# Decoder layer on one core: softmax inverses spread over rows by DMA through DRAM instead of by matmul

## The reference, cut to what matters

```python
qh, kh, vh = (_split_heads(q), _split_heads(k), _split_heads(v))   # 16 heads of 16
scores = jnp.einsum('bhqd,bhkd->bhqk', qh, kh) * scale
attn = jax.nn.softmax(scores, axis=-1)
ctx = jnp.einsum('bhqk,bhkd->bhqd', attn, vh)
ctx = ctx.transpose(0, 2, 1, 3).reshape(x_q.shape[0], x_q.shape[1], D)
return ctx @ W_out.T + b_out
```

## Time and profile before

| | us |
|---|---|
| median of three runs | 714.04 |
| span of the profiled execution, first to last instruction | 712.5 |
| what lies around the span, by that median | 1.5 |
| attention loop, from the first pair's projection to the last scores | 479 to 583 |
| feed-forward, from the first `hidden` to the end | 594 to 712 |

### The profile page before, as it was taken

How to read it: one execution, slowest core, us unless ns; L and a number is a source line. 1 busy time by engine, 2 the same in 40 slices (tenths; PEclk the granted TensorE clock), 3 DMA queues, 4 the chain that set the end, 5 groups by cost and what they waited for, 6 DMA issues and landing times. The chain is left out here.

```text
span 712.5 us, 12566 instructions
## 1 busy us (share of the span) xinstructions
PE 672.1 (94%) x4412; PEld 491.7 (69%) x4412; DVE 633.6 (89%) x1259; ACT 374.0 (52%) x722; POOL 353.7 (50%) x491
## 2 busy tenths in 40 slices
PE   9889999999989998899999799799999999999995
PEld 3478765887747886468886586567877776666664
DVE  4998787999989999989999979748999996999997
ACT  4732157031255503463232633669777776888885
POOL 0633424646135762158451571391692224788785
PEclk9999999999999999999999999999999999999998
DMA  8630045232522436143663065730000000000012
GB/s 311 180 61 1 0 119 104 74 60 25 64 51 38 104 133 60 29 89 60 192 104 74 0 197 88 256 100 2 2 3 2 2 2 1 1 31 31 32 60 90
DMA packets 35353, 50.51 MB, mean 71 GB/s; under 512 B 4857, under 2 KB 29433, under 8 KB 35035
## 3 DMA queue, kind: packets, MB, share of 16 engines
q0 software_dynamic: 7680, 16.77, 15.1%
q1 hardware_dynamic: 26746, 32.15, 13.9%
q10 hardware_dynamic: 864, 0.79, 0.4%
HBM read 29.79 MB, written 7.34 MB: 52 GB/s over the span
## 5 line engine op out<-in xcount | busy, mean ns | idle before, releaser
L744 ACT ACTIVATE yb<-banks 128x256 f32<-128x256 f32 x64 | 24.2, 386 | 149.2 <-PE banks L445 104.1
L470 PE MATMUL banks<-xt_in,w_in 128*128 128x512 f32 x192 | 87.9, 611 | 0.2
L436 PE MATMUL banks<-inv_m,spec_y 128*128 128x256 f32 x384 | 85.5, 379 | 0.0
L390 PE MATMUL banks<-z_cplx,fwd_m 128*128 128x256 f32 x240 | 72.2, 382 | 9.7 <-DVE prod L1130 5.4
L436 PEld LDWEIGHTS banks<-inv_m,spec_y 128*128 128x128 f32 x384 | 73.0, 190 | 9.9
L391 PE MATMUL banks<-z_cplx,fwd_m 128*128 128x256 f32 x240 | 71.4, 379 | 0.0
L470 PEld LDWEIGHTS banks<-xt_in,w_in 128*128 128x128 f32 x192 | 36.7, 194 | 43.3 <-issue 39.8
L390 PEld LDWEIGHTS banks<-z_cplx,fwd_m 128*128 128x128 f32 x240 | 44.8, 190 | 19.0 <-issue 8.4
L391 PEld LDWEIGHTS banks<-z_cplx,fwd_m 128*128 128x128 f32 x240 | 45.6, 190 | 6.2
L1816 ACT ACTIVATE silu<-ps_score,gate_back 128x1024 f32<-128x1024 f32 x32 | 35.6, 1114 | 19.0 <-issue 17.5
L1786 ACT ACTIVATE prob_t<-ps_pt 128x1024 f32<-128x1024 f32 x32 | 32.7, 1022 | 24.1 <-PE ps_pt L1591 24.1
(11 more groups left out here) (299 smaller groups left out, 1726.7 us busy)
## 6 DMA issues: line engine op xcount, KB each, us to landing
x_tok<-in_x SPq DMA_DIRECT2D x8, 512.0 KB, 4.2
x_tok<-in_b_out POOLq DMA_DIRECT2D x8, 512.0 KB, 13.7
v_t<-left POOLq DMA_DIRECT2D x8, 511.5 KB, 4.5
x_t<-left POOLq DMA_DIRECT2D x8, 511.5 KB, 5.3
xt_in<-in_x_t SPq DMA_DIRECT2D x3, 1024.0 KB, 5.9
x_scratch<-x_tok SPq DMA_DIRECT2D x6, 512.0 KB, 4.0
x<-x_scratch SPq DMA_DIRECT2D x6, 512.0 KB, 9.3
out<-x SPq DMA_DIRECT2D x6, 512.0 KB, 2.9
```

The lines of the kernel that those rows point to most:

```text
L390: mm(o, fwd_m[:, at + 2 * half + odd, :], zz[:, 0, :], start=True, stop=False)
L436: last = mm(bank[:, odd * 2 * P:(odd + 1) * 2 * P], spec_y[:, j + odd, part * D + h * P:part * D + (h + 1) * P], inv_m[:, o:o + 2 * P], st ...
L470: last = mm(proj_pair(b, t)[:, c * 512:(c + 1) * 512], w_in[:, k, TILES[t] * P:(TILES[t] + 1) * P], xt_in[:, k, c * 512:(c + 1) * 512], st ...
```

## The change

The inverses no longer go through TensorE. SyncE writes `inv_sum` to a scratch tensor in DRAM (each row four times) and reads it back with each row on 16 partitions, into `inv_all`. ScalarE copies the contexts (`evac_context`) out of PSUM where it copied the spread inverses. The multiplication moves from VectorE to GpSimd (`multiply(i)`). `project(i)` comes a pair later, so residuals and squares do too. GpSimd's order is written anew: bias, multiplications, quantizing and norms take turns. `quantize` is cut into single passes (not shown), two `x_peak` move from the attention loop to steps 0 and 1 of the feed-forward, and the `spread` constant goes (its load not shown).

```diff
@@ -113,14 +113,10 @@
     for r in range(STRIPS):
-        key_head[:, r] = np.arange(STRIP) % HEADS_T == (2 * r + row // NCTX)[:, None]
-    spread = np.zeros((P, STRIPS, P), f)
-    for g in range(STRIPS):
-        spread[g * STRIP:g * STRIP + HEADS_T, g] = row // DH == np.arange(HEADS_T)[:, None]
+        key_head[:, r] = np.arange(STRIP) // REPS == (2 * r + row // NCTX)[:, None]
     out = {
...
         "c_ident": np.eye(P), "c_pairmask": pair_mask, "c_keyhead": key_head.reshape(P, -1),
-        "c_spread": spread.reshape(P, -1),
     }
@@ -1311,14 +1307,18 @@
 X_ROWS = CHUNKS - CHUNKS_B
-X_LATE, X_EARLY = 12, 5
+CHUNKS_EARLY = 4
+X_LATE, X_EARLY = 14, 5
 W_TILE = 11
-X_SLOTS = {3 + n * 5 // 3: n + X_EARLY * CH for n in range(TILES_ALL - X_EARLY * CH)}
+X_LOOP = TILES_ALL - X_LATE
+X_SLOTS = {n: n + X_LOOP for n in range(X_EARLY * CH - X_LOOP)}
+X_SLOTS.update({3 + n * 5 // 3: n + X_EARLY * CH for n in range(TILES_ALL - X_EARLY * CH)})
 HALF = INNER // 2
...
 STRIPS = P // STRIP
+REPS = STRIP // HEADS_T
 FT = INNER // P
@@ -1438,8 +1435,10 @@
         inv_sum = sb("inv_sum", [P, P])
-        inv_all = sb("inv_all", [P, DT * 2 * P])
-        c_t = sb("c_t", [P, DT, 2 * P])
+        late_rows = x_t[:].rearrange("p c t n -> p (c t) n")
+        inv_all, c_raw = late_rows[:, 0:2], late_rows[:, 2:4]
+        c_t = sb("c_t", [P, 2, DT, 2 * P])
+        inv_dram = [nc.dram_tensor(f"inv_scratch_{n}", [P, REPS, P], F32).ap() for n in range(2)]
         row_sum = sb("a_row_sum", [P, 2, CH]); row_var = sb("a_row_var", [P, 2, CH]); spread_sq = sb("a_spread_sq", [P, D])
@@ -1493,7 +1492,7 @@
                 return ps_score[:, INNER + (i - LAST + 1) * 512:INNER + (i - LAST + 1) * 512 + D]
-            return (ps_ctx, ps_inv)[i % 2][:, 0:D]
+            return (ps_inv, ps_ctx)[i % 2][:, 0:D]
@@ -1501,6 +1500,9 @@
+        def ps_project(i):
+            return ps_inv if i == HALVES - 2 else ps_ctx
         def late_order(c):
@@ -1524,6 +1526,21 @@
+            def spread_inverses(i):
+                sp.wait_ge(inverted, i + 1)
+                if i >= 2:
+                    sp.wait_ge(inv_spread, 16 * (i - 1))
+                rows = inv_dram[i % 2]
+                sp.dma_start(rows, inv_sum[:].unsqueeze(1).broadcast_to([P, REPS, P])).then_inc(inv_written, 16)
+                sp.wait_ge(inv_written, 16 * (i + 1))
+                if i >= 2:
+                    sp.wait_ge(ct_ready, i - 1)
+                sp.dma_start(inv_all[:, i % 2].rearrange("p (g n) -> p g n", n=P),
+                             rows.rearrange("(g m) c n -> (m c) g n", g=STRIPS)).then_inc(inv_spread, 16)
...
+            for i in range(HALVES):
+                spread_inverses(i)
             def store(i0, i1):
@@ -1593,26 +1610,20 @@
             def sums(i):
                 pe.wait_ge(pt_evac, 2 * i + 2)
-                pe.wait_ge(inv_evac, i) if i else pe.wait_ge(q_evac, DT * (CHUNKS - Q_EARLY) - 1)
+                pe.wait_ge(inverted, i) if i else pe.wait_ge(q_evac, DT * (CHUNKS - Q_EARLY) - 1)
                 for r in range(STRIPS):
                     for g in range(STRIPS):
-                        k, t = g // DT, g % DT
+                        t, k = g // 2, g % 2
                         last = mm(ps_inv[g * STRIP:(g + 1) * STRIP, 0:P], key_head[:, r, :],
...
-            def spread_inverses(i):
-                pe.wait_ge(inverted, i + 1)
-                for t in range(DT):
-                    for k in range(2):
-                        o = t * 2 * P + k * P
-                        last = mm(ps_inv[:, o:o + P], spread[:, k * DT + t, :], inv_sum[:], start=True, stop=True)
-                last.then_inc(spread_mm, 1)
...
             def values(i):
+                if i >= 2:
+                    pe.wait_ge(added, i - 1)
                 if i:
-                    pe.wait_ge(added, i)
+                    pe.wait_ge(ctx_evac, i)
                 else:
@@ -1625,9 +1636,12 @@
             def project(i):
                 pe.wait_ge(ct_ready, i + 1)
+                pe.wait_ge(inverted, HALVES) if i == HALVES - 2 else pe.wait_ge(ctx_evac, min(i + 2, HALVES))
+                if i == HALVES - 1:
+                    pe.wait_ge(added, HALVES - 2)
                 for k in range(2):
                     for t in range(DT):
-                        last = mm(ps_ctx[:, k * D:(k + 1) * D], c_t[:, t, k * P:(k + 1) * P], wo[:, t, :],
+                        last = mm(ps_project(i)[:, k * D:(k + 1) * D], c_t[:, i % 2, t, k * P:(k + 1) * P], wo[:, t, :],
                                   start=(t == 0), stop=(t == DT - 1))
@@ -1699,12 +1713,11 @@
                 if j % 2 == 0:
-                    if j >= 4:
-                        project(j // 2 - 2)
+                    if j >= 6:
+                        project(j // 2 - 3)
                     if j >= 2:
...
                 elif j >= 3:
-                    spread_inverses(j // 2 - 1)
                     if j == TILES_ALL - 1:
@@ -1716,8 +1729,7 @@
             turn_input(1)
-            project(HALVES - 2)
-            spread_inverses(HALVES - 1)
+            project(HALVES - 3)
             for s in range(TILES_ALL + 3):
@@ -1732,11 +1744,12 @@
                     values(HALVES - 1)
-                if s == 1:
+                    project(HALVES - 2)
+                if s == 2:
                     project(HALVES - 1)
                 if s - 3 in tiles:
-                    if s == 3:
-                        pe.wait_ge(added, HALVES)
+                    if s in (3, 4):
+                        pe.wait_ge(added, HALVES - 4 + s)
                     down(s - 3, FT // 2 if s - 3 == LAST - 1 else 0)
@@ -1786,11 +1799,11 @@
-            def evac_inverses(i):
-                act.wait_ge(spread_mm, i + 1)
-                if i:
-                    act.wait_ge(ct_ready, i)
-                fn(inv_all[:], ps_inv[:], ACT.Copy).then_inc(inv_evac, 1)
+            def evac_context(i):
+                act.wait_ge(pv_mm, i + 1)
+                if i >= 2:
+                    act.wait_ge(ct_ready, i - 1)
+                fn(c_raw[:, i % 2], ps_ctx[:], ACT.Copy).then_inc(ctx_evac, 1)
             def squares(i):
@@ -1857,27 +1870,27 @@
                 if j % 2 and j >= 3:
-                    evac_inverses(j // 2 - 1)
-                if j % 2 == 0 and j >= 6:
-                    squares(j // 2 - 3)
+                    evac_context(j // 2 - 1)
+                if j % 2 == 0 and j >= 8:
+                    squares(j // 2 - 4)
             evac_input(0)
...
             evac_input(1)
-            squares(HALVES - 3)
-            evac_inverses(HALVES - 1)
+            squares(HALVES - 4)
             for s in range(TILES_ALL):
...
                 if s == 0:
-                    squares(HALVES - 2)
+                    evac_context(HALVES - 1)
+                    squares(HALVES - 3)
                 if s - 2 in tiles:
                     evac_hidden(s - 2)
-                if s == 2:
-                    squares(HALVES - 1)
+                if s in (2, 3):
+                    squares(HALVES - 4 + s)
                 if s - 4 in range(LAST - 4):
@@ -1935,8 +1948,12 @@
             pool.wait_ge(ld_kv, 16 * KV_LOADS)
-            for c in range(CHUNKS):
-                add_bias(c)
+            def multiply(i):
+                pool.wait_ge(inv_spread, 16 * (i + 1))
+                pool.wait_ge(ctx_evac, i + 1)
+                if i >= 2:
+                    pool.wait_ge(wo_mm, i - 1)
+                tt(c_t[:, i % 2].rearrange("p t n -> p (t n)"), c_raw[:, i % 2], inv_all[:, i % 2], ALU.mult).then_inc(ct_ready, 1)
             def norm_tile(c, k):
@@ -2020,17 +2041,21 @@
-            norm_chunk(0)
-            pool.wait_ge(w_scaled, 1)
-            quantize(0, w_gate)
-            norm_chunk(1)
-            quantize(1, w_up)
-            quantize(2, w_down)
-            for c in range(2, CHUNKS - 2):
-                norm_chunk(c)
+            for c in range(CHUNKS_EARLY):
+                add_bias(c)
+            for j in range(4, TILES_ALL):
+                if j % 2 == 0:
+                    multiply(j // 2 - 2)
+                    if j < 4 + 2 * (CHUNKS - CHUNKS_EARLY):
+                        add_bias(CHUNKS_EARLY + j // 2 - 2)
+                elif j - W_TILE - 2 in range(18):
+                    quantize((j - W_TILE - 2) // 6, (j - W_TILE - 2) // 2 % 3)
+                if j % CH == 2 and j >= 10:
+                    norm_chunk((j - 10) // CH)
             round_x(0)
...
             back_scales(0)
+            multiply(HALVES - 2)
             round_x(2)
@@ -2041,6 +2066,8 @@
+                if s == 0:
+                    multiply(HALVES - 1)
                 if s in (0, CH):
@@ -2097,15 +2124,8 @@
             def invert(i):
...
                 if i:
-                    dve.wait_ge(spread_mm, i)
+                    dve.wait_ge(inv_written, 16 * i)
                 nc.vector.reciprocal(inv_sum[:], ps_inv[:, 0:P]).then_inc(inverted, 1)
...
-            def normalize(i):
```

(61 more changed lines are left out.)

4 lines of the change are left out of this document (2 added, 2 removed).

## The result

The changed kernel takes 716.53 us (median of seven runs, 715.87 to 719.55) against 714.04 for the one before: ratio 1.0041, 95% interval 1.0026 to 1.0057. It is slower by 2.5 us; the forecast was 2.3. The profiled execution took 718.67 (span 716.9), 2.1 above the median.

A forecast was written before the change was run, and what follows sets the result against it. It took a 7.99 us cycle through TensorE and VectorE to bound the attention loop. With the start's 1.1 gain already counted, 1.6 + 0.5 + 0.2 = +2.3 us on 714.04 gave 716.3 us, range 710.5 to 720.

The forecast's parts named there:

- The ring bounds the loop; spreads and `c_t` are worth nothing: Attention loop: 7.99 us cycle of odd scores, sums, `invert`, even shift sets the pair; removing both pieces gains under 0.1.
- The start, 1.1: First pair, its projection issued a pair later: 6.6 to 6.7 us against 8.0, ScalarE taking 0.2 back; gain 1.1 us.
- 0 for the rest of the loop, 1.2 either way: Twelve attention-loop pairs: removed spreads and `c_t` together change nothing, with 0.1 us a pair, 1.2 us, either way.
- T: Start of the attention loop's last scores: 582.53 before the change, forecast at about 581.4.
- DMA 6.2: Write and read of the inverses through DRAM: 2.6 and 3.4 plus 0.2 for signals, 6.2 us (4.6 to 9.0).
- The hand-over, +1.6: Attention loop to feed-forward: first input tile waits for GpSimd, turned at 590.9 to 591.0 instead of 589.37, +1.6 us.
- Turned input to `hidden(0)`, +0.5: Feed-forward's beginning: 5.0 us instead of 4.47, because the context copy stands ahead of the input copy; +0.5 us.
- `hidden(0)` to `hidden(4)`, 15.7: Feed-forward's first steps: last spread goes, a third projection, residual and two `x_peak` come; 15.7 us against 15.5, +0.2.
- it needs `values` instead of the spread: ScalarE in the loop: swaps one 128x512 copy for another, whose input ends at about the same time; costs nothing.
- the shortening loop (706.7): Rival: VectorE's own sum limits the attention loop, 0.8 us saved a pair, 9.6 in all, total 706.7; chance 0.20.
- The round trip beyond its cover: Rival: inverses' DMAs outlast the loop time hiding them, from 10.8 us; at 13, total about 735; chance 0.08.
- The clock: Rival: TensorE, idling 0.9 in 8 us, drops to 1.2 GHz in the loop; total about 773; chance 0.02.

The follow-up runs named there:

- the first experiment: Changed kernel with round_x(0), round_x(1) and back_scales(0) moved on GpSimd ahead of pair 13's multiplication and the loop's last norm: 713.71 us, ratio 0.9995.

## Why the prediction was right, and where its steps were not

- *The ring bounds the loop; spreads and `c_t` are worth nothing.* Right, shown three ways: ordinary pairs of 8.0 with TensorE idle 0.7 to 0.8 (forecast 0.9) and `prob` as releaser; three quarters of the spreads gone for nothing; VectorE's slot filled for nothing.
- *The start, 1.1.* 1.33 (8.00 to 6.67).
- *0 for the rest of the loop, 1.2 either way.* From 484.45 to T it is 97.63 against 97.11: +0.5. Inside are two pairs longer by 0.68 and 0.49, through `x_unit` beside the multiplication, and ten of 8.05 in the mean, against 8.09 before. The size fell inside my bound; the cause was not in the text. I had costed GpSimd's new work by its room ("per pair 1.2, ... of 8") and never asked beside which VectorE instruction it falls.
- *DMA 6.2.* 2.6 and 2.8; 5.5 us from the write's issue to the multiplication, inside 4.6 to 9.0. The read was over-sized (3.4), because I leaned on the 512 KB loads for its many pieces. The Trainium skill, "DMA: Bandwidth & Descriptors", Anatomy of one DMA — SWDGE (gpsimd) path, gives a fixed 2.0 us plus the bytes at 436 GB/s. An estimate from it is 2.6 for each, and the traces come within 0.2. But that section is on DMAs that GpSimd issues, and these are SyncE's, which the prediction did not say; the nearness is no proof that the formula holds for them.
- *The hand-over, +1.6.* +1.9 (591.29 against 589.37), with every link of the chain as named. T was 0.7 later than I had it, and the multiplication started 0.1 later (585.24 against 585.1) in spite of the quicker DMAs. The squares, priced as the other bound, were only 0.4 behind. The second write's one for one, and the early rounding's full return, show that it is this chain and no other.
- *Turned input to `hidden(0)`, +0.5.* This step failed in the profiled execution: 7.04 instead of 5.0. The 5.0 was laid out at full clock, and there it is right: 4.87 in the first experiment. In the profiled run `values` and `sums` took 0.87 and 0.85 more, and the first `inner` ran slow in part. I had set the fall of the clock beside a stretch busy 18.38 of 22 us and asked it only of the loop, not of the one idle stretch of over 3 us that my own steps contain. The profiled run is 2.1 over the median of its kernel, of the same size. Its mean clock over the run was 0.988 and that of the other long run (719.55) 0.990, against 0.992 to 0.994 in the five from 715.87 to 717.30, so most runs probably keep the clock; their traces were not taken, and this stays an inference. Why some fall and others do not is open.
- *`hidden(0)` to `hidden(4)`, 15.7.* 15.91.
- *ScalarE: "it needs `values` instead of the spread, which end at about the same time in the pair. Nothing."* Right as a sum, too short as a reason. The end of `values` keeps its place only because the spread ahead of it is gone: with a filling there the time grows by 8.4 us, and 5.4 of these go with the filling's place ahead of `values`.
- Of the rivals, the shortening loop (706.7) fell with the first point; its time was not reached, and 708.46, the nearest to it, took reordering four engines. The round trip beyond its cover did not occur, and the doubled write still found the loop covered but for two places. The clock did not fall in the loop (1.00), only at the hand-over.

The median agrees with the forecast to 0.2 us, better than the steps deserve: DMAs taken too long and a start taken too small stood against the longer pairs and a multiplication of 1.28 instead of 1.2.

## What to carry to other kernels

An engine that is busy 94% need not be what the time hangs on: follow one period around the buffers, and cost a removed instruction by where it stands in that ring. When a step is issued a period later, look for the place where the loop ends and the cover with it, and for anything queued behind that step that does not need it: here two roundings and their scales moved ahead gave back all that was lost. Moving work to GpSimd has a second price beside its own duration, in the VectorE instructions that fall on it. The kernel before had one such meeting in its loop (`x_unit` 0.41 at 521.35), the changed kernel two longer ones.
